# Twelve-layer decoder on one core: routing in two steps, four experts on places, and weights of best keys on GpSimd

## The reference

```python
def _L3_ffn_ref(x, w_g, c_fc, c_proj):          # T = 1024 tokens, TOP_K = 2, cap = 320
    logits = xt @ w_g
    top_v, top_i = jax.lax.top_k(logits, TOP_K)
    ...                                          # probs: softmax over the two chosen
    exp_mask = jnp.transpose(one_hot(top_i, N_EXP), (1, 0, 2))
    exp_rank = jnp.cumsum(exp_mask.reshape(TOP_K * T, N_EXP), axis=0) - 1
    exp_mask = exp_mask * (exp_rank < cap)       # all first choices rank ahead of all second ones
    ...
    h = jax.nn.gelu(jnp.einsum('ecd,edf->ecf', exp_batches, c_fc), approximate=False)
    exp_out = jnp.einsum('ecf,efd->ecd', h, c_proj)
    out = cb_weight.reshape(T, N_EXP * cap) @ exp_out.reshape(N_EXP * cap, d)
```

## Time and profile before

| what | us |
|---|---|
| median of three runs | 1427.99 |
| the profiled execution | 1433.34 |
| its span, first to last instruction | 1431.5 |
| TensorE busy, of the span | 1223.0 (85%) |
| VectorE busy | 699.1 (49%) |
| ScalarE busy | 512.5 (36%) |
| GpSimd busy | 424.7 (30%) |
| mean granted TensorE clock, share of 2.4 GHz | 0.885 |
| the last mixture's block | 1314.6 to the end |
| cross-attention of level 0, its turns | about 98 to 160 |
| top attention, its turns | about 400 to 486 |

### The profile page before, as it was taken

How to read it: one execution, slowest core, us unless ns; L and a number is a source line. 1 busy time by engine, 2 the same in 40 slices (tenths; PEclk the granted TensorE clock), 3 DMA queues, 4 the chain that set the end, 5 groups by cost and what they waited for, 6 DMA issues and landing times. The chain is left out here.

```text
span 1431.5 us, 25584 instructions
## 1 busy us (share of the span) xinstructions
PE 1223.0 (85%) x10249; PEld 901.8 (63%) x10249; DVE 699.1 (49%) x2172; ACT 512.5 (36%) x1163; POOL 424.7 (30%) x492
## 2 busy tenths in 40 slices
PE   6999697999867756987897899998989999977884
PEld 5867585788623433674665797785657775565663
DVE  5554533434399254764673316616842125745412
ACT  5533242443265422454354212313433323442321
POOL 7959220000333226754672400003000001041404
PEclk9999798999966677998999659998989988988987
DMA  5000402321290000000000000000021100002112
GB/s 162 1 4 1 181 11 89 89 63 43 110 235 1 1 14 19 1 1 0 1 1 1 9 2 1 1 4 1 2 81 44 30 29 1 2 4 78 68 44 50
DMA packets 52758, 53.07 MB, mean 37 GB/s; under 512 B 19584, under 2 KB 43456, under 8 KB 51616
## 3 DMA queue, kind: packets, MB, share of 16 engines
q1 hardware_dynamic: 51616, 49.33, 11.0%
q0 software_dynamic: 1024, 2.10, 0.7%
HBM read 43.86 MB, written 7.57 MB: 36 GB/s over the span
## 5 line engine op out<-in xcount | busy, mean ns | idle before, releaser
L615 ACT ACTIVATE scratch<-bank 128x512 f32<-128x512 f32 x96 | 52.6, 594 | 93.1 <-PE bank L516 93.1
L574 DVE TENSOR_REDUCE scratch<-bank 128x4 f32<-128x512 f32 x96 | 63.2, 686 | 39.9 <-PE bank L2426 22.2
L439 POOL TENSOR_TENSOR ln_rstd<-ln_ve,ln_half 128x4 f32<-128x4 f32 x28 | 28.7, 1025 | 181.9 <-DVE ln_ve L418 181.8
L2678 POOL TENSOR_TENSOR scratch<-scratch 128x16 f32<-128x16 f32 x16 | 51.7, 3232 | 52.1 <-DVE scratch L3019 52.1
L1061 PEld LDWEIGHTS bank<-scratch 128*128 128x128 f32 x512 | 59.5, 192 | 7.2 <-issue 7.2
L1090 ACT ACTIVATE scratch<-bank 128x512 f32<-128x512 f32 x64 | 38.2, 597 | 67.3 <-PE bank L1051 67.3
L580 DVE TENSOR_TENSOR scratch<-bank,scratch 128x512 f32<-128x512 f32 x96 | 61.4, 681 | 0.0
L1109 DVE SCALAR_TENSOR_TENSOR x_res<-bank,scratch,x_res 128x128 f32<-128x128 f32 x64 | 18.0, 344 | 87.5 <-PE bank L1061 87.5
L516 PEld LDWEIGHTS bank<-ident,scratch 128*128 128x128 f32 x384 | 44.8, 149 | 24.6 <-DVE scratch L580 17.5
L516 PE MATMUL bank<-ident,scratch 128*128 128x128 f32 x384 | 56.0, 292 | 4.7 <-DVE scratch L580 4.7
L1061 PE MATMUL bank<-scratch 128*128 128x128 f32 x512 | 59.6, 275 | 0.0
(11 more groups left out here) (555 smaller groups left out, 3041.8 us busy)
## 6 DMA issues: line engine op xcount, KB each, us to landing
scratch<-conv_kernels SPq DMA_DIRECT2D x8, 1024.0 KB, 11.0
scratch<-e_l_ffn_w SPq DMA_DIRECT2D x20, 256.0 KB, 3.0
scratch<-e_l_ffn_w SPq DMA_DIRECT2D x4, 1024.0 KB, 14.7
values<-scratch SPq DMA_DIRECT2D x8, 512.0 KB, 2.7
scratch<-values SPq DMA_DIRECT2D x8, 512.0 KB, 4.2
weights<-w_l_ffn SPq DMA_DIRECT2D x1, 3698.0 KB, 11.3
scratch<-e_l_ffn_w SPq DMA_DIRECT2D x4, 768.0 KB, 9.3
weights<-w_l_attn SPq DMA_DIRECT2D x1, 2560.5 KB, 8.6
```

The costliest lines, as they stand in the source:

```text
L574: self.nc.vector.tensor_reduce(self.top[:, n % 4, :], self.by_head(self.core.ps[n % 4][:, :]), AX_X, ALU.max, negate=True).then_inc(self.t ...
L615: self.nc.scalar.activation(self.prob_of(n), self.by_head(self.core.ps[4 + n % 2][:, :]), ACT.Exp, scale=scale) \
L2678: nc.gpsimd.tensor_tensor(rn, ss, power, ALU.pow).then_inc(rooted.sem, rooted.up())
```

## The change

**Last mixture.** `LAST` becomes 6: four experts on places, and expert 6 joins the dense ones, so there are 12 jobs: 0 to 3 dense, 4 to 7 on places, 8 to 11 dense; rows on places fall from 1600 to 1280, groups from four to three. Routing is done for first choices as a whole, then for second ones: `dve_pick(k)` replaces one best value a token (the second time in what the first left), and takes the sum over the batches in three instructions over shifted views, with zeros ahead of them that GpSimd sets at the block's start. `pe_counts(k)` is queued behind `up(k)`, ahead of `down(0)`. `dve_place(k)` makes eight columns of `places`; GpSimd waits for each half and issues eight scatters. Two groups are turned ahead of `up(4)`, in two banks, and the third behind it; ScalarE copies them out in place of VectorE. `take_back` of batches 0 to 3 comes between the sums of the last dense jobs, the last job's sum comes after all of them, and SyncE stores each half of x from inside the block.

**Top attention.** `weigh` moves to GpSimd, between L3313 and L3316, with a power of -1 in place of the reciprocal.

**Cross-attention of level 0.** `ahead(n)` comes ahead of "y" in TensorE's program and in `order`.

```diff
-        order += ([("y", n - 2)] if 0 <= n - 2 < B else []) + ahead(n) + ([("o", n - 1)] if 0 <= n - 1 < B else [])
+        order += ahead(n) + ([("y", n - 2)] if 0 <= n - 2 < B else []) + ([("o", n - 1)] if 0 <= n - 1 < B else [])
...
+                for fill in ahead(n):
+                    if fill == ("q", 2, 0):
+                        pe.wait_ge(x_out.sem, x_out.at(1))
+                    project(*fill)
                 if 0 <= n - 2 < B:
...
-                for fill in ahead(n):
-                    if fill == ("q", 2, 0):
-                        pe.wait_ge(x_out.sem, x_out.at(1))
-                    project(*fill)
...
-    FIRST, LAST = 2, 7
+    FIRST, LAST = 2, 6
...
+    def pool(self, pool):
+        self.nc.gpsimd.memset(self.lows, self.LOW).then_inc(self.cleared.sem, self.cleared.up())
+        self.nc.gpsimd.memset(self.zeros, 0.0).then_inc(self.cleared.sem, self.cleared.up())
+
+    def pe_counts(self, pe, k):
+        nc, ones, counts = self.nc, self.core.ones[:, :], self.scores(k)
+        pe.wait_ge(self.picked.sem, self.picked.at(k))
+        nc.tensor.matmul(counts, self.tri, self.picks[k].rearrange("p b e -> p (b e)"), start=True, stop=False)
+        mm = nc.tensor.matmul(counts, ones, self.before[k].rearrange("p b e -> p (b e)"), start=False, stop=(k == 0))
...
+    def dve_pick(self, link, k, values):
+        nc, src = self.nc, self.values if k == 0 else self.left[0]
+        one, two, four = self.sums[k]
+        link(nc.vector.tensor_copy(self.tops[k][:, :, 0], self.top[:, :, k]))
+        for b in range(B):
+            m = nc.vector.match_replace(self.left[k][:, b, :], self.tops[k][:, b, :], src[:, b, :], self.LOW)
+        link(m)
+        link(nc.vector.tensor_tensor(one[:, 4:, :], values, self.left[k][:, :, 0:8], ALU.not_equal))
+        link(nc.vector.tensor_tensor(two[:, 4:, :], one[:, 4:, :], one[:, 3:B + 3, :], ALU.add))
+        link(nc.vector.tensor_tensor(four[:, 4:, :], two[:, 4:, :], two[:, 2:B + 2, :], ALU.add))
+        nc.vector.tensor_tensor(self.before[k], four[:, 4:, :], four[:, 0:B, :], ALU.add) \
+            .then_inc(self.picked.sem, self.picked.up())
+    def dve_place(self, dve, link, k):
+        nc, some, mine = self.nc, slice(self.FIRST, self.LAST), self.of(k)
+        counts, kept, spots = self.by_batch(self.scores(k)), self.kept[k], self.spots[:, self.of(k), :]
+        dve.wait_ge(self.counted.sem, self.counted.at(k))
+        link(nc.vector.scalar_tensor_tensor(out=kept, in0=counts, scalar=self.CAP + 0.5, in1=self.picks[k],
+                                            op0=ALU.is_lt, op1=ALU.mult))
+        link(nc.vector.tensor_tensor(spots, counts[:, :, some], self.first_row[:, mine, :], ALU.add))
+        link(nc.vector.tensor_tensor(spots, spots, kept[:, :, some], ALU.mult))
+        link(nc.vector.tensor_reduce(self.row[:, mine], spots, AX_X, ALU.add))
+        link(nc.vector.tensor_tensor(self.row[:, mine], self.row[:, mine], self.unread[:, mine], ALU.add))
+        nc.vector.tensor_copy(self.core.places[:, mine], self.row[:, mine]).then_inc(self.placed.sem, self.placed.up())
...
-        link(nc.vector.tensor_copy(val, self.by_batch(self.scores())))
-        pick_top(nc, link, val, self.spare, self.top, second, 2, -3.0e38)
-        pick_top(nc, link, val, self.spare, self.top, first, 1, -3.0e38)
-        link(nc.vector.tensor_tensor(second, second, first, ALU.subtract))
-        link(nc.vector.memset(before[0][:, 0, :], 0.0))
-        for b in range(1, B):
-            link(nc.vector.tensor_tensor(before[0][:, b, :], before[0][:, b - 1, :], first[:, b - 1, :], ALU.add))
-        link(nc.vector.tensor_tensor(before[1][:, 0, :], before[0][:, B - 1, :], first[:, B - 1, :], ALU.add))
-        for b in range(1, B):
-            v = nc.vector.tensor_tensor(before[1][:, b, :], before[1][:, b - 1, :], second[:, b - 1, :], ALU.add)
-            if b < B - 1:
-                link(v)
...
+        self.dve_pick(link, 0, scores)
+        self.dve_place(dve, link, 0)
+        self.dve_pick(link, 1, self.left[0][:, :, 0:8])
+        self.dve_place(dve, link, 1)
...
+            for h in range(2):
+                four = slice(4 * h, 4 * h + 4)
+                sp.wait_ge(added.sem, added.at(len(jobs) - 2 + h))
+                sp.dma_start(core.out[:, four, :], x[:, four, :]).then_inc(core.stored, 16)
...
-            pool.wait_ge(route.placed.sem, route.placed.at(0))
-            for b in range(B):
-                for k in range(2):
+            for k in range(2):
+                pool.wait_ge(route.placed.sem, route.placed.at(k))
+                for b in range(B):
...
+                if j < 2:
+                    route.pe_counts(pe, j)
                 if j > 0:
                     down(j - 1)
-                if j == COUNTS_AT:
-                    route.pe_counts(pe)
             down(A - 1)
             turn(0)
+            turn(1)
             for j in range(A, len(jobs) + 1):
                 if j < Z:
-                    pe.wait_ge(emptied.sem, emptied.at(min(j - A, 3)))
+                    pe.wait_ge(emptied.sem, emptied.at(((j - A + 1) * CAP - 1) // (4 * P)))
                 if j < len(jobs):
                     up(j)
-                if j - A < 3:
-                    turn(j - A + 1)
...
+                if j == A:
+                    turn(2)
...
+            def empty(g):
+                act.wait_ge(filled.sem, filled.at(g))
+                n = (groups[g].stop - groups[g].start) * P
+                nc.scalar.copy(takenT[:, 4 * P * g:4 * P * g + n], ps[TURN_BANKS[g]][:, 0:n]) \
+                    .then_inc(emptied.sem, emptied.up())
...
+            add(Z)
+            take_back(0)
+            add(Z + 1)
+            take_back(1)
+            add(Z + 2)
+            take_back(2)
+            take_back(3)
+            add(Z + 3)
...
+            def weigh(b):
+                link(nc.gpsimd.tensor_tensor(weight, tot[:, b % 2, :], tot_left[:, b % 2, :], ALU.subtract))
+                link(nc.gpsimd.tensor_tensor(weight, weight, minus_one, ALU.pow))
+                link(nc.gpsimd.tensor_scalar(weight, weight, core.text_on[:, b:b + 1], 1.0 / H, ALU.mult, ALU.mult))
...
+                    weigh(t - 1)
...
-                    if r == 1 and t > 0:
-                        if t > 1:
-                            dve.wait_ge(kept.sem, kept.at(t - 2))
-                        weigh(t - 1)
```

More of the change, by code:

```diff
@@ L937, in __init__ @@
         self.first_row, self.unread = w.take(2 * B, n), w.take(2 * B)
-        self.both = c.take(2 * B, 8)
-        self.picks = [self.both[:, B * k:B * k + B, :] for k in range(2)]
-        self.spots, self.row, self.given = c.take(2 * B, n), c.take(2 * B), c.take(2 * B)
-        self.placed, self.sourced = core.count("route_chosen"), core.count("route_gates")
-    def by_choice(self, ap):
-        return ap.rearrange("p (k e) -> p k e", e=8)
-    def pe_counts(self, pe):
-        pe.wait_ge(self.picked.sem, self.picked.at(0))
-        for k in range(2):
-            self.nc.tensor.matmul(self.scores(k), self.tri, self.picks[k].rearrange("p b e -> p (b e)"),
-                                  start=True, stop=False)
-            mm = self.nc.tensor.matmul(self.scores(k), self.core.ones[:, :],
-                                       self.before[k].rearrange("p b e -> p (b e)"), start=False, stop=True)
-        mm.then_inc(self.counted.sem, self.counted.up())
+        lows = c.take(2 * B, 16)
@@ new lines, in __init__ @@
+        self.values, tops = lows[:, 0:B, :], lows[:, B:2 * B, :]
+        self.tops = [tops[:, :, 8 * k:8 * k + 8] for k in range(2)]
+        zeros = c.take(6 * (B + 4), 8)
+        self.lows, self.zeros = lows, zeros
+        self.sums = [[zeros[:, (B + 4) * (3 * k + i):(B + 4) * (3 * k + i + 1), :] for i in range(3)] for k in range(2)]
+        self.picks = [self.sums[k][0][:, 4:, :] for k in range(2)]
+        self.left, self.kept = [c.take(B, 16) for _ in range(2)], [c.take(B, 8) for _ in range(2)]
@@ new lines, in __init__, with of @@
+        self.spots, self.row, self.given = c.take(2 * B, n), c.take(2 * B), c.take(2 * B)
+        self.cleared, self.placed, self.sourced = (core.count(f"route_{n}") for n in ("cleared", "chosen", "gates"))
+    def of(self, k):
+        return slice(B * k, B * k + B)
+    def pool(self, pool):
[6 more added lines that the diff above has]
+        mm = nc.tensor.matmul(counts, ones, self.before[k].rearrange("p b e -> p (b e)"), start=False, stop=(k == 0))
+        if k == 1:
+            mm = nc.tensor.matmul(self.by_batch(counts), ones, self.before[0][:, B - 1:B, :].broadcast_to([P, B, 8]),
+                                  start=False, stop=True)
+        mm.then_inc(self.counted.sem, self.counted.up())
@@ L955, in dve @@
     def dve(self, dve):
[L956 to L958 removed]
+        nc, val, prob, kept = self.nc, self.val, self.prob, self.kept
+        scores = self.by_batch(self.scores())
         link = self.link = Link(dve, self.chain)
         self.dve_shift(dve, link)
```

(3 more changed lines are left out.)

103 lines of the change are left out of this document (39 added, 64 removed).

## The result

The changed kernel takes 1421.25 us (median of five runs, 1414.56 to 1422.47) beside 1432.48 us for the kernel before in the same session (1426.39 to 1439.81). The ratio is 0.9913, with a 95% interval of 0.9887 to 0.9939: some 11 us faster, where 21.1 were forecast. The forecast was 1406.9 us, with 1399.0 to 1413.0 as its range.

What follows compares the result with a forecast made beforehand. Bounds: a relay not set by TensorE in the last mixture, TensorE in cross-attention l0, VectorE in top attention. -16.9 - 2.4 - 1.8 = -21.1 us from the median 1427.99 gives 1406.9 us, range 1399.0 to 1413.0.

Steps and rivals of the forecast that it cites:

- The last mixture: Routing, experts on places and tail: earlier writes and one expert fewer on places bring the end 16.9 us earlier.
- the sentence on the dense jobs: Last mixture: dense jobs queued behind the second picks end at 1356.0 instead of 1354.94, before the read-back at 1356.6, costing nothing.
- my cover: Tail of the last mixture: TensorE's dense jobs end at 1407.8, 1.3 us ahead of the last gather.
- rival 4: Tail of the last mixture: TensorE's clock falls and the kernel becomes slower, up to 1453 us; chance 0.03.
- Fills and top attention: Cross-attention of level 0 and top attention: -2.4 us from the fills and -1.8 us from moving the weighing.
- The fills: Cross-attention of level 0: three TensorE waits of 0.81 us behind L356 go, -2.4 us, bounds 0 and -2.5.
- the slack of the loop: Top attention, loop of ScalarE, GpSimd and TensorE: slack 1.7 less 1.18 us leaves 0.5, so the turn becomes 9.2.
- rival 2: Top attention goes at VectorE's pace, turns of 8.1 to 8.6 us, -9.5 to -6.0, about 1401 us; chance 0.13.
- Rival 1: Last mixture: first eight writes stretched 0.28 us each beside VectorE's second picks, 2.2 us, 1409.1 us; chance 0.12.
- The rule of the Trainium skill: Last mixture: VectorE fp32 copies in 2-port mode lock out GpSimd's descriptor writing; two copies cost 0.4 us, sum -20.7.
- Rivals 3 and 5: 3: top attention's turn stays 9.69 us, 1410.4, chance 0.12; 5: a piece of the change fails, about 1418, chance 0.08.
- I am wrong if the last gather does not end the chain: Sign for the end of the last mixture: the last gather, not TensorE, should end the chain.

Runs made afterwards that it cites:

- chip 4: Changed kernel without its sixteen indirect writes, rows read back being zeros: 1415.52 us, ratio 0.9866 to the kernel before.
- the third chip: Unaltered changed kernel rerun there: 1424.88 us beside 1431.28 for the kernel before, ratio 0.995; both kernels had their dense jobs held.
- the chip that holds nothing: Unaltered changed kernel rerun as a control on chip 11: 1414.54 us beside 1432.42 for the kernel before, ratio 0.9858.
- With the writes late: Changed kernel with the first choices' writes held until the second choices' places are there too: 1426.21 us, ratio 0.9962.
- a break: Changed kernel with GpSimd pausing within each row of transfers; after the eighth, by a landing wait 1418.74 us, by a small power 1412.03 or 1417.60 us.

## Why the prediction was wrong

The forecast is 14.3 us below the measured 1421.25. Three pieces make 13.9 of it. Two of them are read from one profile each of before and after; that this is fair is seen from their sum: -5.1 in the last mixture and -6.6 ahead of 500 us make -11.7, where the medians are 11.2 apart. The two profiles are 18.8 apart; 6.2 us of that are a stage that no edit touches (970 us, below).

**The last mixture, +11.8 us.** Forecast -16.9, in the profile on record 115.5 - 110.4 = -5.1. The step that failed is the sentence on the dense jobs: they "end at about 1356.0 instead of 1354.94. That costs nothing". In the table's count this is 40.0; it was 47.3. I priced TensorE's products beside the writes at their rows of before, which came from an execution without a hold. What the runs show in its place is the hold: 7.3 us on the dense jobs, gone when the writes are left out on chip 4, which otherwise holds (39.7). The price itself was right on the chip that holds nothing: 39.7 too. All that hangs on it moved by the same 6 to 8 us: first product on places 48.4 for 42.4, first gather 77.0 for 70.8. Then the second hold took the tail, where my cover was "1.3 us, barely": the last product ended at 106.5, not 91.8, and the end of the chain went from the gathers to TensorE. On the chip that holds nothing, every number of this part stands within 1 us: 39.7, 41.9, 70.6, 90.9, and 99.3 for 98.6.

Nothing in the profile shown could have told me that the hold exists. What it did tell is where the slack went. Before, TensorE was idle for 9.27 us behind the dense jobs, and its last product ended 15 us ahead of the last landing (1410.86 to 1425.95). The change spent both. A hold of 8 us fits into the 9.27, and the kernel before on the third chip does just that: 47.2 for the dense jobs, 115.7 at the end. I treated the cover as free to spend, and put 0.03 on TensorE becoming late (rival 4), by the clock alone; the clock did fall, but in the holds, and took 1.6 and 1.9 us of the miss.

**The base, +4.5 us.** I subtracted from a median of three runs, 1427.99. In the session of the result the kernel before took 1432.48, and 1431.3 to 1434.4 beside the experiments. The profiled execution (1433.34 us) was the better base: less 21.1 it gives 1412.2.

**Fills and top attention, -2.4 us.** Forecast -4.2; the stage behind top attention starts 6.6 us earlier (L439 at 498.1, before 504.7). The fills: 2.8 us, by the L439 rows at 90.55 and 159.75 (90.55 and 162.54 before), forecast 2.4: right, the three waits are gone and a little with them. Top attention: 3.8 us, forecast 1.8. GpSimd's three instructions take 1.71 us with their waits (404.48 to 406.19), forecast 1.82, right. The mis-sized term is the slack of the loop: I took 0.5 us from L3414's idle time and a turn of 9.2; it turned in 8.93, between that and rival 2's 8.1 to 8.6.

Rival 1 is refuted: of the sixteen writes only the first takes 1.26 us, the others 0.95 to 0.97, those beside VectorE's placing and gates (1320.8 to 1323.8) too. With the writes late, when all picks are long done, the first takes 1.27 as well. The rule of the Trainium skill that I weighed there (SBUF — State Buffer, "Who interferes with whom") would have cost 0.4 us. Of the two copies of the second choice one ended 0.8 us ahead of the first write, and the write that started 0.76 us ahead of the other took 0.96. No write is longer, so no run here shows it. Rivals 3 and 5 didn't come. Of the signs that I named, "I am wrong if the last gather does not end the chain" was the one that spoke.

**What hid the miss.** The profiled execution alone came out at 1414.56, only 2.4 us above the 1412.2 that my steps give for it. The windows from 970 to 1034 us, of the changed kernel on record and then of the one on the chip that holds nothing (columns: busy us and instructions of PE, PEld, DVE, ACT, POOL, granted clock, DMA share, GB/s):

```profile
970.00:1034.00 64.00, 58.84 (x567) 35.48 (x565) 50.38 (x117) 28.89 (x58) 8.26 (x6) 1.00 0.01 2
```
```profile
970.00:1034.00 64.00, 61.33 (x467) 36.48 (x468) 45.58 (x104) 24.74 (x49) 8.58 (x7) 0.81 0.01 1
```

This stage is touched by no edit. With TensorE's clock at half for only 1.1 us of it, it takes 64.2 us from L439 row to L439 row; in the eighteen profiles of the experiments the clock falls there for 7.7 to 28.6 us, and it takes 67.1 to 76.3 (70.4 with 15.0 us in the profile of before). That is 3 to 12 us from one execution to the next, as large as the parts of the change; in four of the eighteen a later stage gave 4 to 6 of them back. It is the likely reason why runs of one kernel on one chip lie up to 16 us apart (the changed kernel on the third, 1413.04 to 1429.06). It also blurs the weighing: alone it had won some 5 us at 500 us and nothing at the end; with the fills it was 6.7 at the end. In its profile 1.3 us went back right behind top attention, and the stage at 970 us took 74.6 us, 4.2 more than before. Whether earlier work makes that fall likelier, or it was chance, stays open.

**Open.** What the hold is. Shown is that it goes with GpSimd's indirect transfers: the writes were left out and moved, and the hold with them, while for the gathers it only stands beside them in every profile that has it; that in the changed kernel on record the long one begins some 13 us into a row of writes and ends 2.7 us after the end of the last write; that TensorE's rows come mostly 0.70 us or twice that apart in it; that a break shortens what it costs; and that four sessions had it (among them that of the result), and two, both on chip 11, had not. The profile of before had none either. The Trainium skill (Perfetto Trace Analysis, "Per-engine timelines") draws a stretch between an instruction's push of its semaphore step and its being visible to all engines, and says that it isn't in the profile; it gives no length. Here it is up to 9 us beside the writes and 12.6 beside the gathers. The Trainium skill (NOTIFIC — the notification-queue block, section 7.1) says that the path of the profiler's records can push back on an engine. That rival is untested, and the traces speak for it: sixteen gathers make 256 semaphore steps, and all 256 are recorded in each of the nine profiles without a hold, but only 65 to 105 in each of the eleven with one; it is likewise with the writes. So holds and lost records go together; which of them causes the other, or whether a third thing causes both, isn't shown. Every time given here comes with a clock from such records, so I can't say whether an execution without them is held.

No version beats the changed kernel everywhere: in the profiles, a break wins 4 to 7 us in the last mixture where there is a hold, and loses as much where there is none.

## What to carry to other kernels

Idle time of an engine beside indirect transfers is not free to spend: before moving work into it, ask what the kernel becomes if everything of the other engines that runs beside the row comes 8 to 12 us late, and give that a chance of its own. A profile of one execution on one chip shows one draw; a stage that a second profile shows otherwise (here the clock between 970 and 1034 us, the hold in the last mixture) belongs in the range. And when an experiment cures something, run the uncured kernel on the same chip before believing it.

## What the runs showed of the hardware

- During sixteen indirect transfers issued 1.26 us apart, the semaphore steps of TensorE reached ScalarE and VectorE up to 9 us late (writes) and 12.6 us late (gathers) and in one burst, TensorE's rows came 0.7 us apart or more, and those steps of the transfers that are recorded came on time (the last one 2.09 us after the last write's start, 2.22 without a hold). In some sessions only: the same kernel took 99.3 us for its last mixture on one chip and 110.4 and 112.9 on two others.
- With a hold, 65 to 105 of the 256 steps of sixteen gathers are in the records; without one, all 256.
- Eight writes in a row left the end of the dense jobs where it was on a chip with the hold (39.8 us, 39.7 without it); sixteen delayed it by 7 to 9 us.
- An untouched stage took 64.2 to 76.3 us from one execution to the next, going with how long TensorE's clock stood at the lower level there.
